# Fewer pattern sums on VectorE in a sparse graph kernel: two of four tiles are packed from both pieces

## Chip, cores and metric

One core of a Trainium2 chip runs the kernel. The metric is the device time of one execution in microseconds, the median of several runs. The profile is one further execution.

## What is computed

The inputs are node rows `x` (8192 x 128), a dense 0/1 adjacency matrix (8192 x 8192, float32, about two ones in a row) and weights. Two layers follow each other:

```python
h = maximum(layernorm(x), 0)
x = x + graph_attention(h, adj, weight, att_weight)   # 4 heads, softmax over neighbours
h = maximum(layernorm(x), 0)
agg = adj @ h
msg = relu(agg @ W_msg.T + b_msg)
x = x + gru_cell(msg, h, W_ih, W_hh, b_ih, b_hh)
```

## The kernel before

Reading the adjacency matrix (268 MB) is the large transfer. The kernel reads it once, finds the few ones of each row, and works on lists of neighbours from then on. The 64 tiles of 128 rows form 16 groups of four. A group passes four stages, called c, t, b, g in the code: scan of its tiles; neighbour lists; gathered rows and maxima; weighting, aggregation and the second norm. In each step of the schedule (`body`) one group is scanned while the three groups before it are in the later stages. Every engine has its own hand-written order of calls in `body`; semaphores connect them. Steps 0 and 1 ("early") also build the tables of projected rows (`woven` on VectorE, `turn0` and `project` on TensorE, `turned0` on ScalarE).

A tile is scanned so:

- SP loads it in two pieces (`load`) into the four slots of `adj_in`. A slot comes free when ScalarE has read it. A piece now holds the even or the odd ones of eight planes of 1024 columns, four runs of 4 KB per row.
- ScalarE (`indicate`, L633) turns a piece into 0/1 (second piece: 0/2) in bf16 in `ind`. There are two buffers for first pieces and one, number 2, for second pieces.
- VectorE (`pair`, L1315) adds both pieces of a tile, the pattern sum.
- TensorE (`pack`, L883 and L886) makes two halves of a word array in PSUM: per half one matmul with the word's index and four with powers of two, so that each word holds the bits of eight columns and its place.
- VectorE (`search`, L1323) takes the eight largest words of each of four segments; `decode` splits them.

The order on VectorE in a steady step is: `weigh`, `pair` 0, `search` of the last tile of the group before, `decode`, `add_first` (ends with the variance, L1451), `search` 0, `list_neighbours`, `finish_norm`, `pair` 1, `edges2` (from L1502), `list_edges`, `count2`, `search` 1, `child_logits`, `edge_indices`, `edge_columns`, `pair` 2, `offsets2`, `row_maximum`, `differences2` (from L1491), `search` 2, `edge_logits`, `pair` 3. TensorE: `aggregate`, `pack` 0, `send_lists2` (L976, L978), `list_places`, `pack` 1, `message_columns`, `send_lists`, `message_rows`, `places2`, `rest_logits`, `pack` 2, `maxima`, `neighbours2` (the shift products), `pack` 3. ScalarE works on the eight pieces with its smaller steps between them; `deviation` (L674) is the square root of the norm, `exps` (L670) the exponentials. GpSimd gathers rows.

After the scan a tail of about 256 us ends the lists and does the second layer, group by group.

## Time and profile before

| what | value |
|---|---|
| median of three runs | 1134.26 us (1133.75 to 1134.88) |
| the profiled execution's own time | 1130.72 us |
| its span, first to last instruction | 1128.9 us |
| mean granted clock of TensorE | 0.74 of full |
| moved by DMA | 304.86 MB, 270 GB/s over the span |

The span lies 1.8 us under the execution's own time, and this 3.5 us under the median. A clock of 1.00 is 2.4 GHz, 0.50 is 1.2 GHz. Times in the rows are microseconds from the span's start.

### The profile page before, as it was taken

What the parts mean: (1) busy time and instruction counts of PE and PEld (TensorE: products, weight loads), DVE (VectorE), ACT (ScalarE), POOL (GpSimd) and SP (SyncE); (2) the same over time, 40 slices, a digit from 0 to 9 for tenths busy, and PEclk for the clock granted to TensorE, in tenths of its full rate; (3) what the DMA queues carried; (4) which work ended last, traced back from release to release, by engine and by line L of the source; (5) the groups of instructions that cost most, each with busy time, mean ns of one, the idle gap of its engine ahead of it and who ended that gap; (6) DMA issues with size and microseconds to landing.
All of it is one profiled execution on the core that took longest, in us unless ns stands there. A gap on an engine that the chain in (4) does not pass through costs nothing.

```text
span 1128.9 us, 11717 instructions
## 1 busy us (share of the span) xinstructions
PE 679.9 (60%) x3085; PEld 458.8 (41%) x3085; DVE 866.9 (77%) x3123; ACT 661.4 (59%) x662; POOL 590.4 (52%) x517
## 2 busy tenths in 40 slices
PE   0335455574665655564755656564745575799886
PEld 0224233252443534342443434242533464466543
DVE  8455667788888879797888879797888675377754
ACT  1554574667767585766767685866767143245522
POOL 3011007745537383735546384847466477777771
PEclk9876766777666767767666767667666666799988
DMA  9997889889889898989889899989892011233321
GB/s 297 408 324 275 290 324 367 313 303 389 313 343 358 331 368 312 388 304 393 304 341 355 338 353 349 365 308 397 316 372 93 21 30 46 52 80 84 80 70 47
DMA packets 104867, 304.86 MB, mean 270 GB/s; under 512 B 13793, under 2 KB 31411, under 8 KB 104800
## 3 DMA queue, kind: packets, MB, share of 16 engines
q1 hardware_dynamic: 77088, 274.74, 64.2%
q0 software_dynamic: 17120, 22.56, 7.4%
q10 hardware_dynamic: 10592, 6.82, 2.1%
q8 instruction: 25, 0.41, 0.1%
q14 instruction: 42, 0.34, 0.1%
HBM read 295.65 MB, written 12.71 MB: 273 GB/s over the span
## 4 chain that ended last, share of the span: by engine, by line
DVE 37%; PE 23%; issue 14%; ACT 12%; POOL 10%; DMA 4%; SPq 1%; POOLq 0%; ACTq 0%; DVEq 0%
ACT ind L633 10%; POOL adj_in L583 9%; PE ps L886 5%; DVE cand L1323 5%; PE ps L976 4%; DVE ind L1315 4%; PE ps L978 4%; DVE after_off L1496 3%; DMA adj_in<-in_adj 2%; PE ps L883 2%; DVE own L1368 2%; DVE xb L1442 1%; DVE taken L1335 1%; PE ps L918 1%; PE ps L867 1%
## 5 line engine op out<-in xcount | busy, mean ns | idle before, releaser
L522 POOL DMA_INDIRECT rows_in<-wh_table,idx x192 | 262.6, 1367 | 78.8 <-issue 65.7
L531 POOL DMA_INDIRECT val<-in_adj,val_idx x144 | 163.0, 1132 | 249.3 <-DVE val_idx L1519 209.3
L633 ACT ACTIVATE ind<-adj_in,two 128x4096 bf16<-128x4096 int32 x64 | 237.0, 3703 | 4.1 <-DVE ind L1315 2.9
L633 ACT ACTIVATE ind<-adj_in 128x4096 bf16<-128x4096 int32 x64 | 230.8, 3605 | 14.2 <-ACT t_buf L653 7.0
L883 PE MATMUL ps<-idx_r,idx_w 128*128 128x512 bf16 x128 | 71.4, 558 | 224.7 <-DVE ind L1315 224.7
L886 PE MATMUL ps<-ind,bit_w 128*128 128x512 bf16 x512 | 206.5, 547 | 0.0
L1315 DVE TENSOR_TENSOR ind<-ind 128x4096 bf16<-128x4096 bf16 x64 | 146.5, 2288 | 72.0 <-ACT ind L633 70.9
L583 POOL DMA_INDIRECT adj_in<-g_table,idx x112 | 111.7, 997 | 34.1 <-issue 33.5
L976 PE MATMUL ps<-dsend,after_off 128*128 128x21 f32 x256 | 53.8, 367 | 107.2 <-DVE mv L1451 107.2
L883 PEld LDWEIGHTS ps<-idx_r,idx_w 128*128 128x128 bf16 x128 | 17.7, 138 | 246.4 <-DVE ind L1315 217.2
L886 PEld LDWEIGHTS ps<-ind,bit_w 128*128 128x128 bf16 x512 | 67.4, 132 | 102.4 <-issue 88.2
L976 PEld LDWEIGHTS ps<-dsend,after_off 128*128 128x128 f32 x256 | 52.7, 313 | 113.4 <-issue 113.2
L1323 DVE MAX8 cand<-ps 128x8 f32<-128x256 f32 x256 | 90.4, 415 | 4.8 <-PE ps L886 4.7
L554 POOL DMA_DIRECT2D wh_table<-rows_in x16 | 12.2, 763 | 141.6 <-DVE rows_in L1272 141.6
L674 ACT ACTIVATE sd<-mv,epsc 128x4 f32<-128x4 f32 x16 | 4.7, 296 | 105.0 <-DVE mv L1451 105.0
L978 PE MATMUL ps<-dsend_over,after_off 128*128 128x21 f32 x224 | 49.6, 378 | 0.0
L978 PEld LDWEIGHTS ps<-dsend_over,after_off 128*128 128x128 f32 x224 | 48.8, 327 | 0.0
L1659 DVE SCALAR_TENSOR_TENSOR after_off<-ps,bias_in,after_off 128x512 f32<-128x512 f32 x16 | 12.0, 751 | 46.2 <-issue 31.0
L1648 DVE TENSOR_SCALAR adj_in<-iota,edge_row,val 128x128 f32<-128x128 f32 x128 | 34.9, 360 | 11.1 <-PE ps L1089 10.1
L1087 PE MATMUL ps<-adj_in 128*128 128x128 f32 x224 | 31.0, 289 | 17.2 <-DMA adj_in<-g_table,idx 17.2
L622 ACT ACTIVATE hT<-ps 128x512 f32<-128x512 f32 x16 | 9.4, 592 | 54.2 <-PE ps L859 54.2
L1496 DVE TENSOR_TENSOR after_off<-iota,off 128x1024 f32<-128x1024 f32 x32 | 38.2, 1234 | 0.0
(274 smaller groups left out, 1606.8 us busy)
## 6 DMA issues: line engine op xcount, KB each, us to landing
adj_in<-in_adj SPq DMA_DIRECT2D x128, 2048.0 KB, 9.1
wh_table<-rows_in POOLq DMA_DIRECT2D x16, 264.0 KB, 3.7
g_table<-t_buf ACTq DMA_DIRECT2D x16, 256.0 KB, 8.4
out<-rows_in SPq DMA_DIRECT2D x16, 256.0 KB, 2.5
rows_in<-wh_table,idx POOLq DMA_INDIRECT x192, 5.7
val<-in_adj,val_idx POOLq DMA_INDIRECT x144
adj_in<-g_table,idx POOLq DMA_INDIRECT x128, 2.6
ind<-g_table,idx POOLq DMA_INDIRECT x16, 5.6
```

What stands on the lines that cost most here:

```text
L522: nc.gpsimd.indirect_dma_start(out=rows_in[:, s % 2, t, k, :], out_offset=None, in_=wh_table, in_offset=bass.IndirectOffsetOnAxis(ap=idx[: ...
L531: nc.gpsimd.indirect_dma_start(out=val2[:, s, k:k + 1], out_offset=None, in_=adj_values, in_offset=bass.IndirectOffsetOnAxis(ap=val_idx2[: ...
L583: nc.gpsimd.indirect_dma_start(out=edges_in[:, n % RING2, k, :], out_offset=None, in_=g_table, in_offset=bass.IndirectOffsetOnAxis(ap=idx2 ...
L633: nc.scalar.activation(ind[:, 2 if half else t % 2, :], adj_in[:, slot, :].bitcast(I32), ACT.Relu, bias=two[:, 0:1] if half else 1.0, scal ...
L883: nc.tensor.matmul(o, idx_w[:], idx_r[:, u * HALF:(u + 1) * HALF], start=True, stop=False)
L886: ins = nc.tensor.matmul(o, bit_w[:, k, :], ind[:, t % 2, c0:c0 + HALF], start=False, stop=(k == PAIRS - 1))
L976: nc.tensor.matmul(ps_list2(s)[:, h * 5 + t, :], after_off[:, h, t, :], dsend[:, t, :], start=True, stop=True)
L978: ins = nc.tensor.matmul(ps_list2(s)[:, G, :], after_off[:, n // G, G + n % G, :], dsend_over[:, n % G, :] if n else dsend[:, 0, :], start ...
L1315: V.tensor_tensor(ind[:, t % 2, :], ind[:, t % 2, :], ind[:, 2, :], ALU.add) \
L1323: ins = V.max(cand[:, t, j * 8:(j + 1) * 8], ps[:, (t % 2) * 2 + j // 2, a:b])
L1496: ins = V.tensor_tensor(after_off[:, h], iota[:].unsqueeze(1).to_broadcast([P, 2 * G, P]), off2[:, h].rearrange("p k g -> p (k g)").unsque ...
L1648: V.tensor_scalar(w[:, t, :], iota1[:, t * P:(t + 1) * P], edge_row2[:, q, k:k + 1], val2[:, q, k:k + 1], ALU.is_equal, ALU.mult)
```

## The change

Words of 14 bits in place of 8: 14 planes of 592 columns, the last of 496. A tile's pieces are now contiguous: 4144 and 4048 columns, 7 planes each. The second piece is scaled by 128. Only tiles 1 and 3 of a group (`PAIRED`) get the pattern sum; their packs have one index and seven bit matmuls per half, each 296 columns wide. Tiles 0 and 2 are packed from both pieces: two index matmuls and 14 bit matmuls as soon as the first piece is there, 14 more when the second is. The segments of a search are 148 columns instead of 256. On ScalarE the second piece of tile 1 comes before the square root, the first of tile 2 before the transposed copy as before. A second piece waits for the sum or, where there is none, for the pack of the tile before. The buffers' views and the constants follow the new sizes; the check of empty rows too.

```diff
-BITS = 8
+BITS = 14
 IBITS = 10
-WORDS = N // BITS
+WORDS = 592
 HALF = WORDS // 2
+LAST = N - (BITS - 1) * WORDS
 PAIRS = BITS // 2
 PIECE = PAIRS * WORDS
+CUT = (0, PIECE, N)
+ODD = float(1 << PAIRS)
+PAIRED = (1, 3)
...
                 def load(tile, half, slot):
-                    planes = adj[bass.ds(tile * P, P), :].rearrange("p (k h w) -> p h k w", h=2, w=WORDS)[:, half]
-                    sp.dma_start(adj_in[:, slot, :].rearrange("p (k w) -> p k w", w=WORDS), planes).then_inc(adj_sem[slot], 16)
+                    a, b = CUT[half], CUT[half + 1]
+                    sp.dma_start(adj_in[:, slot, 0:b - a], adj[bass.ds(tile * P, P), a:b]).then_inc(adj_sem[slot], 16)
...
                     if half and tile >= 1:
-                        act.wait_ge(pair_done, tile)
+                        if (t - 1) % G in PAIRED:
+                            act.wait_ge(pair_done, tile // 2)
+                        else:
+                            act.wait_ge(pack_done, tile)
...
-                    nc.scalar.activation(ind[:, 2 if half else t % 2, :], adj_in[:, slot, :].bitcast(I32), ACT.Relu,
-                                         bias=two[:, 0:1] if half else 1.0, scale=-2.0 if half else -1.0,
+                    w = CUT[half + 1] - CUT[half]
+                    nc.scalar.activation(pieces[:, 2 if half else t % 2, 0:w], adj_in[:, slot, 0:w].bitcast(I32), ACT.Relu,
+                                         bias=odd[:, 0:1] if half else 1.0, scale=-ODD if half else -1.0,
...
                         scan(1, 0)
+                    if "c" in do:
+                        scan(1, 1)
                     if "g" in do:
                         deviation(s - 3)
                     if "c" in do:
-                        scan(1, 1)
+                        scan(2, 0)
                     if "g" in do:
                         h2_rows(s - 3)
-                    if "c" in do:
-                        scan(2, 0)
...
                 def pack(s, t):
                     tile = s * G + t
-                    pe.wait_ge(pair_done, tile + 1)
-                    if tile >= 2:
-                        pe.wait_ge(seg_done, tile - 1)
                     for u in range(2):
-                        o = ps[:, (t % 2) * 2 + u, 0:HALF]
-                        nc.tensor.matmul(o, idx_w[:], idx_r[:, u * HALF:(u + 1) * HALF], start=True, stop=False)
-                        for k in range(PAIRS):
-                            c0 = k * WORDS + u * HALF
-                            ins = nc.tensor.matmul(o, bit_w[:, k, :], ind[:, t % 2, c0:c0 + HALF], start=False, stop=(k == PAIRS - 1))
+                        if t in PAIRED:
+                            if u == 0:
+                                pe.wait_ge(pair_done, (tile + 1) // 2)
+                        else:
+                            pe.wait_ge(ind_done, tile * 2 + u + 1)
+                        if u == 0 and tile >= 2:
+                            pe.wait_ge(seg_done, tile - 1)
+                        if t in PAIRED:
+                            o = ps[:, (t % 2) * 2 + u, 0:HALF]
+                            nc.tensor.matmul(o, idx_w[:], idx_r[:, u * HALF:(u + 1) * HALF], start=True, stop=False)
+                            for k in range(PAIRS):
+                                c0 = k * WORDS + u * HALF
+                                ins = nc.tensor.matmul(o, bit_w[:, k, :], pieces[:, t % 2, c0:c0 + HALF], start=False, stop=(k == PAIRS - 1))
+                        else:
+                            for v in range(2):
+                                o = ps[:, (t % 2) * 2 + v, 0:HALF]
+                                if u == 0:
+                                    nc.tensor.matmul(o, idx_w[:], idx_r[:, v * HALF:(v + 1) * HALF], start=True, stop=False)
+                                for k in range(PAIRS):
+                                    c0 = k * WORDS + v * HALF
+                                    w = min(HALF, CUT[u + 1] - CUT[u] - c0)
+                                    ins = nc.tensor.matmul(o[:, 0:w], bit_w[:, k, :], pieces[:, 2 if u else t % 2, c0:c0 + w],
+                                                           start=False, stop=(u == 1 and k == PAIRS - 1))
...
-                    V.tensor_tensor(ind[:, t % 2, :], ind[:, t % 2, :], ind[:, 2, :], ALU.add) \
+                    V.tensor_tensor(pieces[:, t % 2, 0:N - PIECE], pieces[:, t % 2, 0:N - PIECE], pieces[:, 2, 0:N - PIECE], ALU.add) \
                         .then_inc(pair_done, 1)
...
-                    if "c" in do:
-                        pair(s, 0)
...
-                    if early:
-                        pair(s, 2)
...
-                    if "c" in do and not early:
-                        pair(s, 2)
```

## Rows read from the trace of the kernel before

**Rows 1.** The page's totals: busy us, share and instructions; DVE is VectorE, ACT ScalarE.

```profile
PE 679.9 (60%) x3085; PEld 458.8 (41%) x3085; DVE 866.9 (77%) x3123; ACT 661.4 (59%) x662; POOL 590.4 (52%) x517
```

**Rows 2.** Windows by stage: length, engines busy, granted clock, DMA share, GB/s.

```profile
26.00:152.00 126.00, 55.58 (x272) 39.45 (x272) 72.65 (x258) 68.94 (x67) 11.46 (x15) 0.77 0.85 315
152.00:208.00 56.00, 28.28 (x117) 16.88 (x116) 42.59 (x156) 31.52 (x23) 29.30 (x25) 0.62 0.91 344
208.00:873.00 665.00, 396.97 (x1846) 267.90 (x1846) 568.29 (x2120) 465.99 (x390) 370.93 (x292) 0.70 0.89 337
873.00:1129.00 256.00, 196.56 (x841) 132.47 (x841) 161.47 (x482) 92.42 (x179) 168.42 (x166) 0.82 0.22 56
```

**Rows 3.** ScalarE timeline: first pieces of groups 3 and 15 (start, duration).

```profile
208.20 3.60 ACT L633 ACTIVATE ind<-adj_in 128x4096 bf16<-128x4096 int32 x1
...
822.18 3.60 ACT L633 ACTIVATE ind<-adj_in 128x4096 bf16<-128x4096 int32 x1
```

**Rows 4.** VectorE timeline of one steady group; idle time and its releaser in brackets.

```profile
501.17 2.29 DVE L1315 TENSOR_TENSOR ind<-ind 128x4096 bf16<-128x4096 bf16 x1
...
509.50 0.24 DVE L1491 TENSOR_TENSOR dsend<-send,ps 128x84 f32<-128x84 f32 x1 [1.84 <-PE ps L963]
...
512.34 1.41 DVE L1323 MAX8 cand<-ps 128x8 f32<-128x256 f32 x4
...
514.48 2.28 DVE L1315 TENSOR_TENSOR ind<-ind 128x4096 bf16<-128x4096 bf16 x1
...
522.36 2.29 DVE L1315 TENSOR_TENSOR ind<-ind 128x4096 bf16<-128x4096 bf16 x1 [3.69 <-ACT ind L633]
...
538.11 0.74 DVE L1351 MAX8 nbr<-scr 128x8 f32<-128x96 f32 x4
...
542.26 0.23 DVE L1502 TENSOR_SCALAR place<-ps,pid 128x8 f32<-128x8 f32 x1 [0.21 <-PE ps L978]
```

**Rows 5.** ScalarE timeline of the same group.

```profile
514.94 3.60 ACT L633 ACTIVATE ind<-adj_in 128x4096 bf16<-128x4096 int32 x1
...
518.54 3.69 ACT L633 ACTIVATE ind<-adj_in,two 128x4096 bf16<-128x4096 int32 x1
...
525.95 1.28 ACT L674 ACT_TABLE_LOAD   x1
535.12 0.30 ACT L674 ACTIVATE sd<-mv,epsc 128x4 f32<-128x4 f32 x1 [7.88 <-DVE mv L1451]
```

**Rows 6.** TensorE timeline of the same group, and one weight load of a later pack.

```profile
503.92 1.91 PE L886 MATMUL ps<-ind,bit_w 128*128 128x512 bf16 x4
505.63 0.63 PE L883 MATMUL ps<-idx_r,idx_w 128*128 128x512 bf16 x1
...
535.23 3.58 PE L976 MATMUL ps<-dsend,after_off 128*128 128x21 f32 x16 [8.18 <-DVE mv L1451]
...
544.99 1.37 PE L886 MATMUL ps<-ind,bit_w 128*128 128x512 bf16 x4
...
550.22 1.11 PE L905 MATMUL ps<-cm_rest,ownT 128*128 128x70 f32 x8 [0.40 <-DVE cm_rest L1396]
...
876.22 0.15 PEld L886 LDWEIGHTS ps<-ind,bit_w 128*128 128x128 bf16 x1 [0.28 <-issue]
```

**Rows 7.** Windows inside that group (columns as in rows 2).

```profile
505.00:535.00 30.00, 14.26 (x63) 7.89 (x61) 23.58 (x72) 18.68 (x16) 17.87 (x14) 0.73 1.02 393
535.00:541.00 6.00, 5.77 (x28) 5.80 (x28) 5.83 (x30) 5.11 (x6) 0.00 (x0) 0.50 0.48 157
...
524.60:526.70 2.10, 1.99 (x10) 0.89 (x10) 2.03 (x8) 2.08 (x3) 1.79 (x2) 1.00 1.04 390
```

**Rows 8.** First stage: ScalarE's waits for transposes in total, and two single waits.

```profile
ACT hT L622 <- PE ps L859: 54.2, 7, 12.2
...
40.49 0.60 ACT L622 ACTIVATE hT<-ps 128x512 f32<-128x512 f32 x1 [5.46 <-PE ps L859]
...
98.24 2.29 DVE L1315 TENSOR_TENSOR ind<-ind 128x4096 bf16<-128x4096 bf16 x1 [5.90 <-ACT ind L633]
```

More of the change, by code:

```diff
@@ L58 @@
 TW = D + H
-assert WORDS <= 1 << IBITS and BITS + IBITS <= 24 and FIRST_SCAN + SCAN_PRE < NG
+assert WORDS <= 1 << IBITS and BITS + IBITS <= 24 and WORDS == 2 * HALF and 0 < LAST <= WORDS and FIRST_SCAN + SCAN_PRE < NG
 def gat_gru_kernel(nc, x, adj, weight, att, W_msg, b_msg, W_ih, W_hh, b_ih, b_hh, out):
@@ L103, in gat_gru_kernel @@
         bit_w = sb("bit_w", [P, PAIRS, P], BF16)
-        two = sb("two", [P, 1])
+        odd = sb("odd", [P, 1])
         idx_w = sb("idx_w", [P, P], BF16)
@@ L116, in gat_gru_kernel @@
         adj_in = sb("adj_in", [P, SLOTS, PIECE])
-        ind = sb("ind", [P, IND + 1, PIECE], BF16)
+        ind = sb("ind", [P, IND * PIECE + SCAN_PRE * G * D * 2], BF16)
         cand = sb("cand", [P, G, CAND])
@@ L218, in gat_gru_kernel @@
         own2 = adj_in[:, 3, 0:4 * G * G * P // 2].rearrange("p (b h k r) -> p b h k r", b=2, h=2, k=2 * G)
-        edges_scan = ind[:, IND, :].bitcast(F32).rearrange("p (b k d) -> p b k d", b=SCAN_PRE, k=G)
+        edges_scan = ind[:, IND * PIECE:].bitcast(F32).rearrange("p (b k d) -> p b k d", b=SCAN_PRE, k=G)
+        pieces = ind[:, 0:IND * PIECE].rearrange("p (b c) -> p b c", b=IND)
         t_bufs = [rows_in[:, n % 2, :, n // 2, :] for n in range(TBUFS)]
@@ L1195, in _ @@
                 V.memset(ones1[:], 1.0)
-                V.memset(two[:], 2.0)
+                V.memset(odd[:], ODD)
                 V.memset(idx_w[:], 0.0)
@@ L1609, in _ @@
                 weigh(NG - 1, (NG - 1) % 2)
-                pieces = empty[:].rearrange("p (t h) -> p h t", h=2)
-                V.tensor_reduce(over[:, 5:6], pieces[:, 0], AX.X, ALU.max)
-                link(V.tensor_reduce(odd_empty[:], pieces[:, 1], AX.X, ALU.max))
-                link(V.scalar_tensor_tensor(out=over[:, 5:6], in0=odd_empty[:], scalar=0.5, in1=over[:, 5:6], op0=ALU.mult, op1=ALU.max))
+                empties = empty[:].rearrange("p (t h) -> p h t", h=2)
+                V.tensor_reduce(over[:, 5:6], empties[:, 0], AX.X, ALU.max)
+                link(V.tensor_reduce(odd_empty[:], empties[:, 1], AX.X, ALU.max))
+                link(V.scalar_tensor_tensor(out=over[:, 5:6], in0=odd_empty[:], scalar=1.0 / ODD, in1=over[:, 5:6], op0=ALU.mult, op1=ALU.max))
                 link(V.tensor_reduce(over[:, 0:5], checks[:], AX.X, ALU.max))
```

13 lines of the change are left out of this document (8 added, 5 removed).

## Prediction

> **What bounds the kernel now.** I read the page's totals first [rows 1]: VectorE is busy 866.9 us of 1128.9, more than any other engine. Such a share averages over stages, so the stages come next [rows 2]: start-up, a first stage in which the tables are built beside the first eight tiles (26 to 152 us), one group of transition (to 208), the steady groups (208 to 873), and a tail without scan (256 us). The change touches the first four of them. In the steady stage VectorE is busy 568.3 of 665 us and ScalarE 466.0, and the DMA engines show a share of 0.89 at 337 GB/s.
>
> The steady groups are alike. ScalarE's first piece of group 3 starts at 208.20, that of group 15 at 822.18 [rows 3], so a group takes 613.98 / 12 = 51.17 us. The order within one is read from the VectorE timeline of the group that begins at 514.48 with the pattern sum of the last tile [rows 4]. I call this time zero (T0). VectorE then runs nearly without a pause to 565.6; it stands twice: 3.69 us before the sum at 522.36, for ScalarE's second piece, and 1.84 us at 509.50, for TensorE's shift products, which stand behind the third tile's pack. The chain alternates between engines: sum of tile 3, logits and exponentials, two ScalarE pieces (514.94 to 522.3) [rows 5], sum of tile 0 (to 524.57), search, decode, add_first (variance at 535.1), 7.0 us of list products on TensorE (535.23 to 542.26) [rows 6], edges, lists, sum of tile 2 (501.17), pack, maxima, shift products, differences, search.
>
> The DMA engines are the second bound, not far away. From 505 to 535 they are full: share 1.02 at 393 GB/s. From 535 to 541 they fall to 0.48 [rows 7], since ScalarE stood 7.88 us before its square root [rows 5] and freed no slot. A group moves 337 GB/s x 665 us / 13 = 17.2 MB; at 393 GB/s that is 43.9 us.
>
> **The change part by part, in a steady group.**
>
> *Sums of tiles 0 and 2 removed:* 2 x 2.29 us of VectorE [rows 4], and for tile 0 the 3.69 us wait before it.
>
> *Searches over 148 columns instead of 256.* The four searches of a tile take 1.41 us for 256 columns; four of the same operation over 96 columns, of another array, take 0.74 [rows 4]. Between the two lies 0.67 us for 640 columns, so at 148 columns a tile's four take 0.74 + 208 x 0.00105 = 0.96: 0.45 us less per tile, 1.8 per group. Bounds: nothing, if the array in PSUM has the price of 256 for less too, and 0.60 a tile, if the time is all in proportion.
>
> *Matmuls.* In a pack now four of 512 columns start at 503.92 and the next thing at 505.63 [rows 6]: 427 ns each, which is 512 columns at 1.2 GHz, the lower level. After 524.6 the granted clock is 1.00, and ten take 1.99 us [rows 7], the upper level. A matmul of 296 columns is then 247 or 124 ns. A summed tile has 16 of them, 3.95 us at the lower level against 4.27 now. An unsummed tile has 30, 7.3 us at the lower, 3.7 at the upper level. Twenty more weight loads per such tile cost nothing where they lie under a running matmul: the load at 876.22 takes 0.15 us and starts with the matmul that runs to 876.65 [rows 6]. Without this cover each costs 0.15 us.
>
> *The pieces* are 4144 and 4048 columns instead of twice 4096: ScalarE's sum is unchanged. The sum of two pieces is 0.03 us shorter.
>
> *ScalarE's order.* The second piece of tile 1 now comes before the square root. It must wait for the end of tile 0's pack, which empties its buffer. Behind it stand the root, the rows, and VectorE's finish_norm.
>
> *SP's transfers* keep their number and bytes; one contiguous run per row replaces four of 4 KB.
>
> Now one group, worked from T0 = 0, where the sum of tile 3 starts.
>
> 1. Sum to 2.2; TensorE packs tile 3 from 2.3 for 3.95 us, to 6.3. VectorE weighs meanwhile (its wait began at 522.36 - 3.69 = 518.67, so that is over at 4.2) and searches from 6.5. Now it searches after tile 0's sum, at 10.1 (522.36 + 2.2).
> 2. From there to the variance, where ScalarE's 7.88 us end, are 10.5 us (524.6 to 535.1 [rows 5]), less 0.45: variance at 16.55, now 20.6.
> 3. TensorE runs the aggregate, 3.5 us at most (its pack of tile 3 ended 4.27 us after 516.8, the next pack starts at 524.6), to 9.8. Then tile 0's pack, whose pieces ScalarE gave at 4.3 and 8.1 [rows 5]. It follows the aggregate, after which the level is the upper one now [rows 7]; I take 3.8 us: 13.6. ScalarE: second piece of tile 1 13.8 to 17.5, table load and root 1.6: 19.1. VectorE asks for the root after the last maxima of list_neighbours, now 3.75 us after the variance (538.85), so at 19.85. The later root costs nothing; without this cover it would cost 2.5.
> 4. List products start at 16.7 and take 7.03: edges at 23.7. VectorE had 0.21 us to spare there [rows 4].
> 5. From edges to the rest logits on TensorE are 7.96 us (542.26 to 550.22 [rows 6]), less a search: 31.2. They take 1.1: 32.3.
> 6. Here TensorE takes over: the pack of tile 2 needs 7.3 us at the lower level, 6.1 if it rises midway, as tile 1's did (1.37 us for its last four, at 544.99, against 1.91). Its first piece is there, the second comes at 34. From a pack's end to the shift products are 1.6 us now (503.6 + 4.3 to 509.5): 41.2, or 40.0. VectorE's own work is done 3.2 or 2.0 us earlier; the wait of 1.84 us grows. So the second sum's 2.2 us are mostly exchanged for a longer pack.
> 7. Differences, search, logits: 509.50 to 514.48 is 4.98, less 0.45. The next T0 is at 45.7, or 44.5. ScalarE's last piece follows tile 2's pack and the copy of the maxima and ends at 43.6 to 44.8, just in time.
>
> A group is thus 44.5 to 45.7 us by the engines, 43.9 by DMA. Two bounds so close hinder each other, so I take 45.6: a gain of 5.57 us, 13 times (last sums of groups 2 to 15): 72.4 us. Of it 3.6 are the wait and sum before tile 3's search, 1.35 the three searches on the path, 0.6 the rest.
>
> *The first stage.* ScalarE stands seven times, 54.2 us in all, before a tile's first piece, for transposes that TensorE makes after the first half of the pack of the tile before [rows 8]. Four of these come behind unsummed tiles (0, 2, 4, 6); the first is 5.46 us, the longest 12.20. That half now starts when the first piece is done, not after second piece (0.60 of copy and 3.7 later) and sum (2.4): 6.7 earlier, but 16 matmuls of 247 ns for 5 of 427 take 1.8 longer. Net 4.9 us on four tiles, 20 us. Bounds: 12 (if VectorE's tables, woven in between, hold it) and 26 (tile 4: VectorE also stood 5.90 us for its sum ahead of a decode [rows 8]). It holds as long as DMA keeps up: 315 GB/s x 126 us = 39.7 MB, at 393 that is 101 us, 25 less than now.
>
> *Tail.* Unchanged but for one search: 0.5 us.
>
> Sum: 72.4 + 20 + 0.5 = 93 us. The profiled execution took 1130.72 us (span 1128.9), so 1038; the median of the runs is 3.5 us above it: 1134.3 - 93 = 1041 us.
>
> **Rivals.**
>
> *DMA binds* (0.17). The group ends at its floor plus stalls, 46.6 to 47.5 us: 13 x 4.1 + 16 + 0.5 = 70, so 1064. For it: the floor is only 1.1 us under the path, and gathers share the engines. Against: four slots are issued 8 us or more ahead of use in the working above. The Trainium skill ("DMA: Bandwidth & Descriptors", How a descriptor splits into AXI transactions) says a descriptor that does not start 256-byte-aligned needs an extra transaction; the second piece starts at byte 16576, which is not aligned. For runs of 4 KB that would be 17 for 16 on half the bytes, an estimate of a floor of 45.3; no row here shows it.
>
> *The waits only move* (0.10). TensorE stays at the lower level in the unsummed packs. Tile 0's then ends at 17.1, ScalarE's second piece of tile 1 at 21.0 and the root at 22.6, 2.7 us after VectorE asks, of which the list products hide some; tile 2's takes the full 7.3: 45.7 + 2.0 = 47.7 a group. With the first stage at its lower bound 13 x 3.47 + 12 + 0.5 = 57.6: 1077 us. For it: the clock is at 0.50 whenever a pack follows a pause (503.92). Against: the pack that follows the aggregate is at the upper level now [rows 7].
>
> *Slower, by weight loads that do not hide* (0.05). With matmuls of 247 ns in place of 427, each load of 0.15 us [rows 6] shows. On the path stand 46 matmuls (tiles 3 and 2): 7.0 us; tile 0's pack (30 x 0.15 = 4.5 later, behind 2.4 of tile 3's) delays the root by 1: 53.6 a group. 13 x 2.43 = 32 us more, and the first stage gains 20 - 4 x 2.4 = 10: 1156 us. It turns the sign from 93 / (13 x 46 + 4 x 16) = 0.14 us unhidden per matmul. Against: the spacing in a pack is exactly that of the columns, and a load lies under each matmul [rows 6]. The Trainium skill ("TensorE: Matmul & The Clock Gate", The mechanism) states that weight loads overlap running matmuls only when they use different row groups, which these do not; by that rule this rival would hold. The trace's row speaks against it.
>
> *No effect beyond noise* (0.03): part of the unhidden loads, 0.14 us per matmul, eats what the sums give: 1134.
>
> *Better than forecast* (0.05): the first stage gives 26 and groups take 44.2, near the DMA floor: 13 x 6.97 + 26 + 0.5 = 117, so 1017.
>
> **Numbers.** The forecast case has 0.60, with 1024 to 1060 (group 44.6 to 46.6, first stage 12 to 26). The range takes in DMA binding and most of the moved waits: 1022 to 1080. A measurement of this kernel tells 0.2%, 2.3 us, from no change. Faster 0.92, same 0.02, slower 0.06.
>
> **What would show it.** 64 sums become 32; VectorE's wait before the remaining ones for ScalarE vanishes, a wait of about 2.3 us for TensorE appears before tile 3's search; the shift products' wait is 2 to 3.2 us; groups are 45 to 46 us apart; steady DMA reaches 375 GB/s or more; spacing in a pack is 247 or 124 ns. Wrong would be: a spacing near 0.4 us, ScalarE waiting for adjacency transfers, or a square root that ends after list_neighbours.

## The result, and the profile of the changed kernel

The changed kernel takes 1018.7 us (median of 4 runs, 1017.0 to 1021.6) against 1134.0 us for the kernel before (4 runs): a ratio of 0.899, interval 0.897 to 0.901. The prediction was 1041 us with a range of 1022 to 1080. The direction was right, the size was not: the kernel is 22 us faster than forecast and lies just under the range. This holds where the kernel before takes 1134 us. On three of the four chips of the experiments it takes 1237 to 1254 us, and on the two of these that ran the changed kernel unedited that one is 12% *slower* (1388.5 against 1238.5 us, 1386.0 against 1237.3); the experiments come to it.

The page's totals of the changed kernel, beside [rows 1]:

```profile
PE 693.8 (68%) x3917; PEld 540.9 (53%) x3917; DVE 764.3 (75%) x3097; ACT 660.1 (65%) x662; POOL 537.9 (53%) x517
```

VectorE has 102.6 us less to do, in a span that is 113.7 us shorter (1015.2). The windows by stage, beside [rows 2] (us; busy us of PE, PEld, DVE, ACT, POOL; granted clock, DMA share, GB/s):

```profile
26.00:133.00 107.00, 59.54 (x370) 47.97 (x370) 64.24 (x263) 70.16 (x68) 11.43 (x15) 0.81 0.97 377
133.00:189.00 56.00, 26.95 (x168) 21.24 (x168) 33.00 (x148) 28.07 (x21) 29.38 (x28) 0.68 0.81 328
189.00:761.00 572.00, 412.35 (x2522) 340.95 (x2522) 485.52 (x2096) 464.80 (x393) 319.54 (x289) 0.74 0.97 391
761.00:1015.00 254.00, 192.39 (x847) 128.72 (x847) 160.80 (x481) 92.42 (x179) 168.62 (x166) 0.84 0.22 57
```

The steady stage is 572 us instead of 665, and TensorE's granted clock in it is 0.74 instead of 0.70 although it has 676 more products. The stage's ends are the last sums of groups 2 and 15, on the VectorE timeline:

```profile
189.17 2.26 DVE L1342 TENSOR_TENSOR ind<-ind 128x4048 bf16<-128x4048 bf16 x1
...
760.72 2.26 DVE L1342 TENSOR_TENSOR ind<-ind 128x4048 bf16<-128x4048 bf16 x1
```

So 13 groups take 571.55 us, 43.96 each, against 51.17. They are less alike than those before, from 43.2 to 45.1 us. The one shown, from T0 = 541.66, is the shortest (43.19); where the usual one differs, the text on the prediction says so. VectorE first, the rows that answer to [rows 4]:

```profile
541.66 2.26 DVE L1342 TENSOR_TENSOR ind<-ind 128x4048 bf16<-128x4048 bf16 x1
...
548.25 0.98 DVE L1350 MAX8 cand<-ps 128x8 f32<-128x148 f32 x4 [2.42 <-PE ps L900]
...
562.57 2.26 DVE L1342 TENSOR_TENSOR ind<-ind 128x4048 bf16<-128x4048 bf16 x1
564.75 0.22 DVE L1529 TENSOR_SCALAR place<-ps,pid 128x8 f32<-128x8 f32 x1
...
580.38 0.24 DVE L1518 TENSOR_TENSOR dsend<-send,ps 128x84 f32<-128x84 f32 x1 [1.66 <-PE ps L987]
...
584.85 2.26 DVE L1342 TENSOR_TENSOR ind<-ind 128x4048 bf16<-128x4048 bf16 x1
```

The second row is at +6.6, where step 1 put it (6.5), after the wait of 2.42 us that was forecast as 2.3. The searches take 0.97 us (0.96 forecast). TensorE's timeline of the same group, beside [rows 6]:

```profile
552.57 2.77 PE L909 MATMUL ps<-ind,bit_w 128*128 128x296 bf16 x21
558.48 2.33 PE L1000 MATMUL ps<-dsend,after_off 128*128 128x21 f32 x16 [3.15 <-DVE mv L1478]
...
572.33 1.11 PE L929 MATMUL ps<-cm_rest,ownT 128*128 128x70 f32 x8
573.27 0.29 PE L905 MATMUL ps<-idx_r,idx_w 128*128 128x296 bf16 x1
573.40 1.04 PE L909 MATMUL ps<-ind,bit_w 128*128 128x296 bf16 x7
574.28 0.29 PE L905 MATMUL ps<-idx_r,idx_w 128*128 128x296 bf16 x1
574.41 2.77 PE L909 MATMUL ps<-ind,bit_w 128*128 128x296 bf16 x21
578.77 1.06 PE L942 MATMUL ps<-pm,own 128*128 128x8 f32 x8 [1.60 <-DVE pm L1438]
```

Seven products start within 0.88 us (573.40 to 574.28), some 125 ns apart: tile 2's pack runs wholly at the upper level and is over at 577.2 after 3.9 us. Step 6 had given it 6.1 to 7.3. What comes next waits 1.60 us for VectorE, not for the pack. In ten of the thirteen groups this pack takes 3.9 us at a granted clock of 1.00; in the other three it takes 4.8, 5.2 and 5.0 at 0.75 to 0.82. The second of these, in the group from T0 = 277.41:

```profile
309.70 1.96 PE L929 MATMUL ps<-cm_rest,ownT 128*128 128x70 f32 x8
...
311.70 1.93 PE L909 MATMUL ps<-ind,bit_w 128*128 128x296 bf16 x7
```

Here the rest logits already run at the lower level (1.96 us for what takes 1.11 above), as do the first products of the pack (1.93 for 1.04). The maxima follow the pack without a pause, and the group takes 45.07 us. ScalarE's order, beside [rows 5]:

```profile
555.38 3.67 ACT L642 ACTIVATE ind<-adj_in,odd 128x4048 bf16<-128x4048 int32 x1 [2.36 <-PE ps L909]
...
560.45 0.30 ACT L683 ACTIVATE sd<-mv,epsc 128x4 f32<-128x4 f32 x1
```

The wait of 7.88 us before the root is gone. Full stretches of the DMA engines (410 to 426 GB/s), beside [rows 7], carry more than the 393 GB/s on which the floor of 43.9 us rested; at 420 GB/s 17.2 MB take 41 us:

```profile
515.00:530.00 15.00, 14.57 (x79) 12.71 (x79) 14.02 (x71) 10.24 (x12) 4.46 (x5) 0.63 1.01 426
```

And ScalarE's waits for the transposes of the first stage, beside [rows 8]: 26.4 us instead of 54.2.

```profile
ACT hT L627 <- PE ps L868: 26.4, 6, 7.2
```

### The profile page after: what moved, and what is told of

It is laid out like the page before. It is cut to its first block, busy times and chain, and to the rows that moved or that the text cites. A ratio compares the mean times of both kernels' runs of the same rounds, so it can differ in the third digit from the quotient of the medians.

```text
span 1015.2 us, 13355 instructions
## 1 busy us (share of the span) xinstructions
PE 693.8 (68%) x3917; PEld 540.9 (53%) x3917; DVE 764.3 (75%) x3097; ACT 660.1 (65%) x662; POOL 537.9 (53%) x517
## 4 chain that ended last, share of the span: by engine, by line
DVE 43%; PE 26%; POOL 12%; issue 9%; DMA 5%; ACT 4%; ACTq 0%; POOLq 0%; DVEq 0%
POOL adj_in L588 11%; PE ps L900 6%; DVE ind L1342 4%; DVE cand L1350 4%; PE ps L1000 4%; PE ps L1002 4%; DMA x<-in_x 3%; DVE after_off L1523 3%; ACT ind L642 2%; PE ps L909 2%; DVE own L1395 2%; DVE xb L1469 2%; PE ps L942 1%; DVE scr L1360 1%; DVE taken L1362 1%
## 5 line engine op out<-in xcount | busy, mean ns | idle before, releaser
L527 POOL DMA_INDIRECT rows_in<-wh_table,idx x192 | 226.3, 1179 | 79.5 <-issue 68.2
L536 POOL DMA_INDIRECT val<-in_adj,val_idx x144 | 146.1, 1015 | 208.6 <-DVE val_idx L1546 168.7
L642 ACT ACTIVATE ind<-adj_in,odd 128x4048 bf16<-128x4048 int32 x64 | 234.6, 3666 | 26.5 <-PE ps L909 20.8
L642 ACT ACTIVATE ind<-adj_in 128x4144 bf16<-128x4144 int32 x64 | 233.3, 3646 | 11.0 <-ACT t_buf L662 7.0
L909 PE MATMUL ps<-ind,bit_w 128*128 128x296 bf16 (+1 forms) x896 | 129.2, 299 | 1.7 <-ACT ind L642 1.7
L900 PE MATMUL ps<-ind,bit_w 128*128 128x296 bf16 x448 | 115.8, 431 | 0.0
L897 PE MATMUL ps<-idx_r,idx_w 128*128 128x296 bf16 x64 | 27.5, 429 | 120.6 <-DVE ind L1342 120.6
L909 PEld LDWEIGHTS ps<-ind,bit_w 128*128 128x128 bf16 x896 | 91.3, 102 | 30.5 <-ACT ind L642 1.9
L1350 DVE MAX8 cand<-ps 128x8 f32<-128x148 f32 x256 | 61.8, 304 | 34.8 <-PE ps L900 34.4
L900 PEld LDWEIGHTS ps<-ind,bit_w 128*128 128x128 bf16 x448 | 63.8, 142 | 37.1
L1342 DVE TENSOR_TENSOR ind<-ind 128x4048 bf16<-128x4048 bf16 x32 | 72.3, 2260 | 8.2 <-ACT ind L642 8.2
L1000 PEld LDWEIGHTS ps<-dsend,after_off 128*128 128x128 f32 x256 | 47.8, 287 | 50.9 <-issue 50.8
L1002 PE MATMUL ps<-dsend_over,after_off 128*128 128x21 f32 x224 | 47.6, 368 | 0.0
L1680 DVE SCALAR_TENSOR_TENSOR after_off<-ps,bias_in,after_off 128x512 f32<-128x512 f32 x16 | 12.0, 751 | 46.5 <-issue 33.0
L1669 DVE TENSOR_SCALAR adj_in<-iota,edge_row,val 128x128 f32<-128x128 f32 x128 | 34.8, 362 | 12.9 <-PE ps L1113 11.9
```

Source lines behind the costliest of these rows:

```text
L527: nc.gpsimd.indirect_dma_start(out=rows_in[:, s % 2, t, k, :], out_offset=None, in_=wh_table, in_offset=bass.IndirectOffsetOnAxis(ap=idx[: ...
L536: nc.gpsimd.indirect_dma_start(out=val2[:, s, k:k + 1], out_offset=None, in_=adj_values, in_offset=bass.IndirectOffsetOnAxis(ap=val_idx2[: ...
L642: nc.scalar.activation(pieces[:, 2 if half else t % 2, 0:w], adj_in[:, slot, 0:w].bitcast(I32), ACT.Relu, bias=odd[:, 0:1] if half else 1. ...
L897: nc.tensor.matmul(o, idx_w[:], idx_r[:, u * HALF:(u + 1) * HALF], start=True, stop=False)
L900: ins = nc.tensor.matmul(o, bit_w[:, k, :], pieces[:, t % 2, c0:c0 + HALF], start=False, stop=(k == PAIRS - 1))
L909: ins = nc.tensor.matmul(o[:, 0:w], bit_w[:, k, :], pieces[:, 2 if u else t % 2, c0:c0 + w], start=False, stop=(u == 1 and k == PAIRS - 1))
```

## The experiments

Sixteen edited kernels in five series, and the changed kernel itself twice more; kernels of one series ran on one chip beside the kernel before, and ratios are to that. Group times are from variance to variance. In the first four series something came up that none of the theories had: in the changed kernel and most of its variants, TensorE, VectorE and ScalarE are held up together, for some 10 to 20 us in nearly every group. "Hold-up" below means that. `...` marks what is cut from the code.

**Series 1 (kernel before 1248.0 us): the parts of the change.** The kernel before, with each piece one contiguous run (the factors of the second piece follow):

```
   ...
-  planes = adj[...].rearrange("p (k h w) -> p h k w", h=2, w=WORDS)[:, half]
+  sp.dma_start(adj_in[:, slot, :], adj[bass.ds(tile * P, P), half * PIECE:(half + 1) * PIECE]) ...
```

> The kernel before with one thing changed: the two pieces of a tile are the left and the right 4096 columns, one run of 16 KB per row instead of four of 4 KB (second piece scaled by 16). Theory A (the engines' chain sets a steady group of 51.17 us, transfers do not): groups stay at 51.0 to 51.3 us, total 1126 to 1135 us; full windows rise from 393 to above 410 GB/s. Theory B (transfers already held the kernel before, and longer runs are a good part of the gain): groups fall below 50 us, total under 1120.

Measured: 1261.0 us, ratio 1.010 (1.005 to 1.016). Eight of its twelve steady groups, one behind the other, have no hold-up and take 51.2 to 51.3 us, as those before: contiguous runs alone bring nothing to a group. Full stretches reach 411 to 415 GB/s, as forecast. The last two groups take 52.7 and 54.9 us; more of the 1% can't be placed, as there is no trace of the kernel before from this chip.

The changed kernel with all four sums (`PAIRED = (0, 1, 2, 3)`) and ScalarE's old order:

> The changed kernel with words of 14 bits and contiguous pieces, but all four tiles get the pattern sum and ScalarE has its old order. Three searches on the path save 0.45 us each and two packs 0.3 each: groups of 49.2 us, total about 1104 us (1095 to 1112) if the sums that go (and the wait before tile 0's) are the main part of the gain. If width and transfer were the main part, groups would be near 45 and the total under 1050.

Measured: 1287.2 us, 1.036 (1.028 to 1.043). Groups of 54 to 57 us are held up; two of twelve are not and take 50.7, where 49.2 was forecast. So searches of 148 columns with all sums kept are worth some 0.5 us a group, by these two, and not the 2 us expected. What a group gains beyond that comes with the two sums taken out or with ScalarE's new order; no run without hold-ups tells these apart.

The changed kernel with ScalarE's old order (the root before the second piece of tile 1, and so on down):

```
+  if "g" in do:
+      deviation(s - 3)
   if "c" in do:
       scan(1, 1)
   if "g" in do:
-      deviation(s - 3)
+      h2_rows(s - 3)
   if "c" in do:
       scan(2, 0)
-  if "g" in do:
-      h2_rows(s - 3)
```

> The changed kernel with ScalarE's square root again ahead of the second piece of tile 1. That piece then starts at the variance, 16.9 us after the sum of tile 3, and not at 13.7, and ends at 20.7; VectorE's sum of tile 1 starts at 20.9 now. Forecast: 0 to 0.4 us more per group, total 1019 to 1026 us. If the order is what lets the transfers run on, the DMA share falls well under 0.97 and groups reach 45.5, total 1040.

Measured: 1396.1 us, 1.122 (1.115 to 1.128). And with each piece loaded as four runs per row instead of one:

```
-  sp.dma_start(adj_in[:, slot, 0:b - a], adj[bass.ds(tile * P, P), a:b])
+  n = (b - a) // 4
+  sp.dma_start(adj_in[:, slot, :].rearrange("p (k w) -> p k w", k=4)[:, :, 0:n],
+               adj[bass.ds(tile * P, P), a:b].rearrange("p (k w) -> p k w", k=4)) ...
```

> The changed kernel with each row's part cut into four runs of 4144 (4048) bytes, by a gap of some columns between quarters in the slot; everything else as it is. Theory A (engines set the 43.9 us group, transfers only nearly): at the rate of the kernel before (393 GB/s full) a group needs 43.9 us of transfer, so groups of 44.0 to 44.6, total 1019 to 1028. Theory B (the long runs made room and without them transfers bind): 45 to 46.5 a group, total 1033 to 1052, with ScalarE waiting for adjacency transfers.

Measured: 1388.9 us, 1.115 (1.109 to 1.122). Both were to lie near 0.9. Instead a group took 61 to 63 us, and the last four 66 to 67. Neither tells about its own question here; together they show that the hold-up needs neither ScalarE's new order nor the long runs.

**Series 2 (kernel before 1238.5 us, another chip): is it the changed kernel itself?**

> The changed kernel once more, unedited, as the base of this series: the four kernels of the series before ran where the kernel before itself took 1248 instead of 1134 us, with every engine's next instruction now and then about 1.2 us late. If that belongs to the place and not to the kernels, this run gives 1017 to 1022 us beside 1134 for the kernel before, or again a ratio far from 0.90 beside 1248.

Measured: 1388.5 us, 1.122 (1.119 to 1.126), groups 61.4 us and the last four 66 to 67. The same kernel as in the result. Three edits of it:

```
   ins = V.max(cand[:, t, j * 8:(j + 1) * 8], ps[:, (t % 2) * 2 + j // 2, a:b])
+  if t == 2:
+      ins = V.max(again[:, j * 8:(j + 1) * 8], ps[:, (t % 2) * 2 + j // 2, a:b])
```

> The changed kernel with the four searches of tile 2 done twice (the second result goes to a spare array): 0.9 us more of VectorE work per group, between the shift products and the sum of tile 3. Theory A (the engines' chain still sets the group): 0.9 x 13 = 12 us more, 1030 to 1033 us. Theory B (transfers set it, share 0.97 in the steady stage): under 4 us more.

Measured: 1400.5 us, 12.0 more, of 16 x 0.97 = 15.5 added. Theory A had 12 more as well, though from 1019 us.

Tile 2's pack made twice (its 30 products again before `pack_done`):

> The changed kernel with tile 2's pack done twice, 30 more matmuls, so that it takes about as long (7.4 us at the upper clock level) as I forecast for the lower level (7.3). TensorE had 1.6 us in hand there. Theory A: the forecast's error was this pack's level alone, so the group comes to 43.9 + 3.7 - 1.6 = 46.0 us, total 1042 to 1050, the first stage some 3 us more. Theory B (the group is set elsewhere, by transfers or VectorE): the total stays under 1030.

Measured: 1451.8 us, 63 more, of about 16 x 3.7 = 59 at the upper level; theory A had 23 to 31, with 1.6 us a group hidden.

Three quarters of each piece loaded (from the third tile on a quarter of the patterns is stale, and the kernel's last test of the values is left out):

```
+  if tile >= 2:
+      b = a + (b - a) * 3 // 4
   sp.dma_start(adj_in[:, slot, 0:b - a], adj[bass.ds(tile * P, P), a:b])
```

> The changed kernel with only three quarters of each piece loaded from the third tile on (the rest of the slot keeps older data, so the edges found are not the right ones; the last of the seven checks before the tail is left out so that the same path is taken). Theory A: transfers are covered, the group stays at 43.5 to 43.9 us, 0 to 6 us less in the steady stage, and up to 8 less in the first: 1005 to 1019. Theory B (transfers bind): groups fall below 43, total under 1000.

Measured: 1381.1 us, 7 less. So where groups are held up, added work on the engines' chain shows nearly in full or more, and a quarter of the loads hardly at all. How much of the 63 is a longer hold-up, brought by the added products, these runs don't tell.

What the hold-up looks like, on the timeline of all engines of the unedited changed kernel in series 2:

```profile
478.76 0.21 DVE L1506 TENSOR_SCALAR late_place<-base,pid_low 128x1 f32<-128x1 f32 x1 [0.73 <-DVE base_early L1505]
...
479.47 0.29 PE L909 MATMUL ps<-ind,bit_w 128*128 128x296 bf16 x1 [0.88 <-issue]
...
480.18 0.30 PE L909 MATMUL ps<-ind,bit_w 128*128 128x296 bf16 x1 [0.42 <-issue]
...
480.90 0.29 PE L909 MATMUL ps<-ind,bit_w 128*128 128x296 bf16 x1 [0.43 <-issue]
...
500.26 0.24 DVE L1518 TENSOR_TENSOR dsend<-send,ps 128x84 f32<-128x84 f32 x1 [13.86 <-remote]
```

TensorE starts one product every 0.71 us instead of every 0.124, for nothing that the profile shows, and later ones 1.4 or 2.1 us apart; VectorE's step that waits for the operation before it on the same engine comes 0.73 us late as well. Each instruction itself takes its usual time. The windows around it (columns as above) show what goes ahead:

```profile
470.00:478.00 8.00, 6.95 (x58) 5.98 (x57) 7.55 (x45) 5.06 (x6) 6.03 (x6) 1.00 0.59 225
478.00:500.00 22.00, 5.38 (x22) 3.78 (x20) 2.62 (x15) 3.96 (x4) 14.99 (x15) 0.62 0.60 222
```

172 instructions in 8 us, and then 76 in 22 us, 15 of them GpSimd's gathers at their own pace. Where the changed kernel takes 1019 us, the same stretch (569 to 577, 185 instructions) is followed by no such thing.

**Series 3 (kernel before 1237.3 us, a third chip): TensorE's instructions?**

> The changed kernel, unedited, once more, as the measure for the three beside it. Theory I (the loss on the two earlier chips goes with the number of instructions that TensorE is given, 13355 against 11717): where the kernel before takes some 1240 us, this one takes some 1390 us, and the lengthened groups show short instructions of three engines 0.7 to 1.4 us apart. Rival II (the loss goes with the unsummed packing's waits and order, whatever the count): the same here. Where the kernel before takes 1134 us, both say about 1019 us.

Measured: 1386.0 us, 1.120. Words of 8 patterns (`BITS = 8`, `WORDS = 1024`), 18 products per unsummed pack instead of 30:

> The changed kernel with words of 8 patterns and 1024 columns in place of 14 and 592: two contiguous pieces of 4096 columns, VectorE's sum for tiles 1 and 3 alone, ScalarE's new order, but an unsummed pack has 18 products (16 of 512 columns) where it has 30 (28 of 296), a summed one 10 where it has 16, and the search reads 256 columns at a time where it reads 148. Theory I: 56 packing products per group instead of 92, some 570 fewer in all, so where the changed kernel takes 1390 us this one is 40 to 60 us faster in spite of the longer search (0.4 us x 4 per tile, about 1.6 us on the chain of tile 3 and as much on tile 2's). Rival II: 1390 us or, with the search, up to 1430 us. Where nothing stalls, both say slower than the changed kernel by 2 to 4 us per group, 1050 to 1080 us.

Measured: 1408.1 us, 1.138 (1.134 to 1.142), where theory I had 40 to 60 us less than the changed kernel's 1386. The kernel before, each packing product as two of 256 columns:

```
   ...
+  for y in range(2):
+      c = c0 + y * HALF // 2
+      ins = nc.tensor.matmul(o[:, y * HALF // 2:(y + 1) * HALF // 2], bit_w[:, k, :], ind[:, t % 2, c:c + HALF // 2], ...)
```

> The kernel before with each packing product of 512 columns made as two of 256: the same columns, 8 more TensorE instructions per tile, 512 more in all, and nothing else changed. Theory I: where the kernel before takes some 1240 us this one takes 30 to 50 us more. Rival II: no change there beyond 5 us, since TensorE has as much work as before and no wait is moved. Where the kernel before takes 1134 us both say within 5 us of it.

Measured: 1242.3 us, 1.004 (1.001 to 1.006). No sums at all (`PAIRED = ()`):

> The changed kernel with no sum on VectorE at all: all four tiles of a group are packed from both pieces, 120 packing products per group instead of 92, 4.5 us less on VectorE. Theory I: about 450 more TensorE instructions, so 30 to 50 us more than the changed kernel where that takes 1390 us. Rival II: also more, since two more packs are in the new form, by 0 to 60 us. Where nothing stalls: edge work of VectorE begins 2.3 us earlier but tiles 1 and 3 are packed 2 to 4 us longer, so 0 to 3 us per group either way, 1000 to 1060 us.

Measured: 1316.1 us, 1.065 (1.061 to 1.070). Theory I falls three times over: fewer TensorE instructions are slower, 1024 more (512 products, each with its weight load) cost 5 us, and the version with the most is 70 us faster than the changed kernel. (The 13355 and 11717 that it names are the instructions of all engines; TensorE's products are 3917 and 3085.) In the trace of the halved products steady groups take 51.0 to 52.1 us, 51.4 on the mean; its 115 us over the span of the kernel before (1128.9) come before group 15's first piece (about 11) and behind it (about 103), where one wait of VectorE alone has 66.1. So what the kernel before loses on these chips, it loses mostly behind the scan.

**Series 4 (kernel before 1253.9 us, the chip of series 2): gathers, or the sum of all events?** GpSimd issues 21 gathers in a row, 27.3 us, and in the window above the hold-up began while they ran and ended 3 us after them. Two kernels leave the nine gathers of adjacency values out, with what hangs on them:

```
-  for k in range(E2):
-      nc.gpsimd.indirect_dma_start(out=val2[:, s, k:k + 1], ..., in_=adj_values, ...).then_inc(values_in[s % 2], 16)
```

> The changed kernel without GpSimd's nine gathers of adjacency values per group (the weights that hang on them are then zero, and the check of them is out): GpSimd's burst of gathers is 12 long instead of 21, 15.6 us instead of 27.3. Nothing on the group's chain waits for these gathers. Theory G (where the changed kernel takes 61 us per group, its engines are held up while GpSimd's gathers run, from some 8 us after the first to some 3 us after the last): the hold-up of a group falls from 17 us to at most 6, a group takes 44 to 51 us, and the kernel 1150 to 1260 us. Theory R (it goes with the dense stretch of all engines, whatever the gathers do): 60 us per group and 1370 us or more. If no hold-up is left, the group shows the time of the chain itself: 43 to 44.5 us if it is the engines' chain that sets it.

Measured: 1146.1 us, 0.914 (0.907 to 0.920). In its profiled execution (span 1159.1, longer than the median) eight of twelve groups take 44.7 to 47.6 us and four 51 to 55: fewer are held up, and for less long.

> The kernel before without the same nine gathers per group (and without what hangs on them). Theory G: its groups of 51.2 us stay as they are, since nothing is held up in them here; 5 to 60 us less outside them (first groups and tail, where the same kernel takes 100 us more here than in the traces of before). Theory R: the same 51.2 us, and nothing gained elsewhere beyond 10 us. Against it the kernel above shows what the change is worth where the gathers are out: ratio 0.89 to 0.93 if nothing is held up, near 1.1 if theory R holds.

Measured: 1213.2 us, 0.969 (0.962 to 0.975), groups 50.8 to 51.3. With the gathers out on both sides the changed kernel is the faster one on this chip too, 1146.1 / 1213.2 = 0.945. And the kernel before with idle events on SyncE:

```
   load(n // 2, n % 2, n % SLOTS)
+  for _ in range(25):
+      sp.sem_inc(extra, 1)
```

> The kernel before with 25 semaphore increments more on SyncE behind each of 124 adjacency loads, 200 per group, on a semaphore that nobody waits for: no engine, no transfer and no wait is touched. Theory R in its strongest form (what holds the engines up is the number of instructions and events of the whole core): groups go from 51.2 to 55 us or more, 60 us or more in all. Theory G: within 6 us of the kernel before.

Measured: 1338.1 us (four runs, 1316.3 to 1355.5), 84 more than the kernel before and at least 62, by the lowest. It now is held up too: its first eight groups alternate between 66 and 53 us. No engine that works and no transfer was touched. So both theories hold a part: gathers taken out shorten the hold-up, and increments added elsewhere bring it about. Each added increment is an instruction of SyncE and a semaphore event in one, and a gather brings 16 increments with it; that it is the sum of such things over the whole core is a reading of these runs, not shown, and the size did not follow a plain count, as series 3 shows.

**Series 5 (kernel before 1133.2 us, a fourth chip): what sets a group.** No hold-up here. All three leave the value gathers out, and no run on this chip leaves out only them; they are compared with the changed kernel of the result. The 45.0 us from which their expectations start came from the chip of series 4 and is some 1 us high. Tile 2's first piece packed a second time:

```
   ...
+  for y in range(2 * (u and t == 2)):
+      o = ps[:, (t % 2) * 2 + y, 0:HALF]
+      nc.tensor.matmul(o, idx_w[:], idx_r[:, y * HALF:(y + 1) * HALF], start=True, stop=False)
+      for k in range(PAIRS): ...
```

> The changed kernel without the nine gathers of adjacency values (as in the kernel without values, 1146 us), and tile 2's first piece packed a second time between its two pieces: 16 products more, about 2 us at TensorE's upper clock level and 4 at the lower. Theory C (the engines' chain through tile 2's pack, the maxima, the shift products and search 2 sets the group, and the forecast's 2.4 to 3.6 us too much for this pack at the lower level were 2.4 to 3.6 us too much for the group): the groups that aren't held up go from 45.0 to 46.5 to 47.2 us. Theory D (the adjacency loads set them, the chain has slack here): 45.0 to 45.5 us.

Measured: 1019.8 us, 0.898 (0.895 to 0.901). Ten of twelve steady groups take 42.6 to 44.2 us, like the changed kernel's, where theory C had 46.5 to 47.2. So 2.0 us more of TensorE are nearly all hidden, in the 1.60 us that it waited for VectorE: the maxima now follow the pack without a pause and come hardly later, at +37.1 to +38.2. The other two groups take 47.0 and 47.4.

> The same kernel without values, and from the third tile on only three quarters of each adjacency piece are loaded (a quarter of the patterns is then stale; 12.9 MB per three groups instead of 17.2 per group in proportion). Theory D: groups that aren't held up fall from 45.0 us to 42 us or less. Theory C: they stay at 44.3 to 45.0 us.

Measured: 1009.5 us, 0.890 (0.888 to 0.892); groups 42.7 to 43.8 us, and two of 47.0 and 47.1, 43.9 on the mean as in the changed kernel. (Its estimate of 12.9 MB is for one group, as the 17.2 are.) A quarter less to load does not shorten a group: theory D, with 42 us or less, falls; theory C's 44.3 to 45.0 are missed too, by some 1 us, the error of their base. Its two kinds of group show what TensorE's level does. TensorE's timeline of the rest logits (L925) and tile 2's pack in a long one (47.1 us, list products from 331.3):

```profile
347.74 1.96 PE L925 MATMUL ps<-cm_rest,ownT 128*128 128x70 f32 x8
...
349.74 1.93 PE L905 MATMUL ps<-ind,bit_w 128*128 128x296 bf16 x7
...
351.71 4.18 PE L905 MATMUL ps<-ind,bit_w 128*128 128x296 bf16 x21
355.73 0.98 PE L938 MATMUL ps<-pm,own 128*128 128x8 f32 x8
...
392.72 1.11 PE L925 MATMUL ps<-cm_rest,ownT 128*128 128x70 f32 x8
...
393.79 1.04 PE L905 MATMUL ps<-ind,bit_w 128*128 128x296 bf16 x7
...
394.80 2.77 PE L905 MATMUL ps<-ind,bit_w 128*128 128x296 bf16 x21
399.07 1.06 PE L938 MATMUL ps<-pm,own 128*128 128x8 f32 x8 [1.51 <-DVE pm L1434]
```

and, in the last four rows, in the next (43.4 us, from 378.3). The windows of the two packs (TensorE alone, granted clock behind it):

```profile
349.50:355.90 6.40, 6.40 (x34) 0.60 0.93 303
393.70:397.60 3.90, 3.86 (x32) 1.00 0.35 81
```

Same kernel, same work: at the lower level but for its last part the pack takes 6.4 us and the maxima follow without a pause, 24.5 us after the list products began; at the upper one it takes 3.9 and they come at 20.7, after a wait for VectorE. VectorE then waits 4.94 us for the shift products in the long one (1.66 in the other), and the groups differ by 3.65 us. Not all of this is the pack's: in the long group TensorE is at the lower level from the list products on, so the pack starts 18.2 us after them instead of 15.3. Of the 3.7 us by which the maxima are later, 2.9 come from the products ahead of the pack and the rest from the pack, whose 2.4 us more are partly taken up by the wait of 1.51.

No sums, without value gathers:

> The same kernel without values, and without any sum on VectorE: tiles 1 and 3 are packed from both pieces too. VectorE's edge work no longer waits for tile 1's sum (2.26 us), search 3 waits for 28 products of which the first 14 can lie beside ScalarE's second piece. By theory C groups that aren't held up fall from 45.0 to 43 to 44.5 us; if TensorE's longer packs for tiles 1 and 3 cost more than VectorE gains, they are 45 to 47 us. Since TensorE is given 28 products more per group, a hold-up may come in more of the groups.

Measured: 978.8 us, 0.864 (0.862 to 0.866), the fastest of all. Its steady groups take 42.9 us on the mean (first pieces of groups 3 and 15 on ScalarE), where the kernel just above takes 43.9 and theory C had 43 to 44.5; of the 31 us between these two, 17 are there when the steady groups begin. Now the transfers are the bound (window of its steady stage, columns as in the stage windows):

```profile
190.00:705.00 515.00, 415.60 (x2675) 333.94 (x2674) 391.00 (x1893) 425.66 (x354) 181.59 (x160) 0.82 1.00 410
```

and ScalarE waits 64.1 us for adjacency loads in the whole trace, 51.8 of them in this stage, where it waited 5.8 and 2.8 in the changed kernel.

## Why the prediction was wrong

*First stage and transition: right.* The last sum of group 2 starts at 189.17 instead of 207.9: 18.7 us, forecast 20.

*Steps 1 to 3 of the group: right.* Search 3 at +6.6 (6.5), variance at +16.7 (16.55), packing products 247 and 124 ns apart with all weight loads hidden, tile 0's pack at the upper level in 3.9 us (3.8), the root not late.

*Step 4: right in most groups.* The list products were to take 7.03 us; seven of the thirteen groups have 6.9 to 7.0, and there edges come at +23.7 to +23.8 (23.7). In the group shown they take 5.75, as part of them still runs at the upper level; the mean is 6.6. VectorE's remaining sum then ends at 564.83 and holds edges at +23.1, so only part of it counts.

*Step 5: right.* Rest logits at +30.7 (31.2), at +31.4 in the usual group.

*Step 6 failed.* It said that TensorE takes over, since tile 2's pack needs 6.1 to 7.3 us at the lower level. In ten of thirteen groups of the changed kernel it runs at the upper one and takes 3.9. It then is no longer on the path: VectorE's own work reaches the maxima later, and the wait in front of them is 1.60 us of slack for TensorE. In the group shown the maxima come at +37.1 and the next T0 at +43.2. In the usual one, with the list products as forecast, they come at +37.8 and +43.9, where 38.4 to 39.6 and 44.5 to 45.7 were forecast. The wait for the shift products, which was to grow to between 2 and 3.2 us, is 1.66.

What the level of this pack alone is worth can be bounded. In series 5 a pack of 5.9 us that starts on time costs almost nothing, for it fills the wait of 1.60. Packs of 6.1 to 7.3 would put the maxima 0.6 to 1.8 us later than the +37.8 of the usual group: an estimate, but just what separates 44.5 to 45.7 from 43.9. The longer groups are no clean test of it, since in them TensorE is at the lower level ahead of the pack too. The two with a pack of 4.8 and 5.2 us take 45.0 and 45.1 us, with rest logits at +32.7 and +32.3; the third slow pack (5.0 us) starts nearly on time, and its group takes 43.9; the pair in series 5 differs by 3.65 us, most of it from ahead of the pack.

The level was taken from a pack that TensorE begins out of a pause, the wait for tile 2's sum, on TensorE's timeline before, just ahead of the first row of [rows 6]:

```profile
503.52 0.61 PE L883 MATMUL ps<-idx_r,idx_w 128*128 128x512 bf16 x1 [3.56 <-DVE ind L1315]
```

In every steady group before it begins after such a pause, at a granted clock of 0.50 to 0.58. Now that sum is gone: from 564.9 to 577.2 TensorE has work without a pause, and the pack begins at the level of the products ahead of it. That the missing pause is what keeps the level up fits these rows but is not shown, for a run of work without a pause can stay low too: in the long group of series 5 TensorE works from 331.3 to 357.2 without one, and its level rises only within the pack.

*The DMA floor, and the 1.1 us that I added for two close bounds.* The floor of 43.9 us came from 393 GB/s; full stretches of the changed kernel reach 410 to 426, a floor of about 40 to 42. (It is not the long runs alone: with four runs per row full stretches carry 411 and 412, in series 1.) ScalarE waits 2.8 us in all for adjacency loads in the thirteen groups, and with a quarter of the loads gone a group keeps its 43.9 us. So nothing was to be added.

In the sum: 13 x 7.2 = 93.6 instead of 72.4 for the steady groups, 18.7 instead of 20, and 1.3 instead of 0.5 for the tail: 113.6 instead of 93. The mis-sized term is the first, by 1.64 us a group: 0.54 lie under the lower end of step 7, 44.5, which has the pack at 6.1 us, and 1.1 are the choice of 45.6 above that end. How the 7.2 us are shared among the sums, the searches and ScalarE's order is read from the traces; no run without hold-ups takes back one of them alone.

*The rivals.* DMA binding (1064) did not come; the rule on descriptors that start off a 256-byte boundary (the Trainium skill, "DMA: Bandwidth & Descriptors", How a descriptor splits into AXI transactions) speaks of a cost that did not show: the second pieces, which start at byte 16576, arrive in packets of 16192 bytes that take 605 ns in the trace, 26.8 bytes per ns, and the first pieces, which start with the row, in packets of 16576 bytes that take 622, 26.6. With four runs per row, off such a boundary too, they take 158 ns for 4048 bytes, 25.6, against 159 for 4096 in the kernel before, 25.8. Unhidden weight loads (1156) did not come either: 28 products of 296 columns under 28 weight loads keep to 124 ns, so the rule that loads overlap only across row groups (the Trainium skill, "TensorE: Matmul & The Clock Gate", The mechanism) does not describe this trace. "Better than forecast" had the right time (1017) and half of the right reason: groups of 44, but a first stage of 18.7, not 26.

*What I had no case for:* that the sign depends on the chip that the kernel runs on.

## What to carry to other kernels

Before pricing a step at TensorE's lower level, ask whether the change itself fills the pause in front of it: here the sum that stood ahead of the pack was gone, the level stayed up, and 30 products took 3.9 us where 6.1 to 7.3 had been set. A step that got longer may still have slack; look for what its successor waits for, and let groups of one trace that differ in TensorE's level serve as the experiment, after a look at where the level first differs. And run on more than one chip before a change that raises the number of instructions and semaphore events per microsecond is called a gain. The version to try next is the one without sums: it beats the changed kernel by 5% where there are hold-ups (1316 against 1386 us); where there are none it took 979 us, but without the value gathers, and its time with them was not measured there.

## What the runs showed of the hardware

On three chips (series 1 to 4) TensorE, VectorE and ScalarE are held up together, while GpSimd's gathers keep their 1.30 us: instructions of TensorE start 0.71, 1.4 or 2.1 us apart, semaphores are seen 0.7 us and more late, while each instruction and each DMA packet takes its usual time. Shown: 200 idle semaphore increments per group on an otherwise idle engine bring it about in the kernel before (+84 us by the medians), and 9 gathers fewer per group take most of it away (1146 against 1388 on the same chip). Ruled out: the number of TensorE instructions alone, the long adjacency runs, ScalarE's new order. The instruction loads are the same in both places too: the trace has 32 packets of one instruction queue with a median of 0.98 us with hold-up and 1.07 without. What stays open is the resource. The traces from these chips also hold fewer semaphore events for the same kernel, 6242 against 13300 in all for the changed one, so the recording itself may take part in it. The halved products, with no hold-up in their steady groups, have few as well (7768; the kernel before has 13380 where there are no hold-ups), so the missing events go with the chip and not with a hold-up. No run here separates the recording from the program's own events.
